# Layer norms of the graph front and behind the experts: the normalizing pass moved from VectorE to ScalarE

## What is computed

```python
def _layernorm(x, axis=-1, eps=1e-05):
    m = jnp.mean(x, axis=axis, keepdims=True)
    v = jnp.var(x, axis=axis, keepdims=True)
    return (x - m) / jnp.sqrt(v + eps)
...
x = x + _L0_gnn_ref(_layernorm(x), ...)   # three graph layers over 40000 edges
x = x + _L0_ffn_ref(_layernorm(x), ...)   # 16 experts, 3 chosen per token, and a shared one
x = x + _L1_gnn_ref(_layernorm(x), ...)   # graph convolution and kernelized attention
x = x + _L1_ffn_ref(_layernorm(x), ...)   # sparse choice of 128 of 1024
```

## Time and profile before

| | |
|---|---|
| median of three runs | 1318.26 us (1315.52 to 1320.05) |
| the profiled execution | 1312.12 us |
| its span, first to last instruction | 1310.4 us |
| TensorE busy (matmuls) | 1233.0 us, 94% |
| VectorE busy | 530.4 us, 40% |
| ScalarE busy | 442.3 us, 34% |
| GpSimd busy | 196.8 us, 15% |
| granted TensorE clock, mean | 0.984 of full |

### The profile page before, as it was taken

How to read it: one execution, slowest core, us unless ns; L and a number is a source line. 1 busy time by engine, 2 the same in 40 slices (tenths; PEclk the granted TensorE clock), 3 DMA queues, 4 the chain that set the end, 5 groups by cost and what they waited for, 6 DMA issues and landing times.

```text
span 1310.4 us, 19216 instructions
## 1 busy us (share of the span) xinstructions
PE 1233.0 (94%) x6568; PEld 820.9 (63%) x6569; DVE 530.4 (40%) x1399; ACT 442.3 (34%) x933; POOL 196.8 (15%) x209
## 2 busy tenths in 40 slices
PE   4999899999999899989999999999989999989797
PEld 3555485566456555468877887786565586564465
DVE  8999532111134335100000000001395355667894
ACT  7878532121212110011111111111122442338893
POOL 1000000000000007411111111111363000104480
PEclk9999999999999999999999999999999999989899
DMA  9200000000020110572164312664462000200011
GB/s 226 80 1 1 1 2 1 1 1 1 1 100 30 63 66 1 177 260 72 44 234 160 131 48 63 221 232 165 152 183 88 17 17 2 73 1 1 1 31 50
DMA packets 42977, 98.25 MB, mean 75 GB/s; under 512 B 4142, under 2 KB 6632, under 8 KB 41874
## 3 DMA queue, kind: packets, MB, share of 16 engines
q1 hardware_dynamic: 28642, 68.70, 15.7%
q0 software_dynamic: 6144, 16.45, 4.5%
q10 hardware_dynamic: 8112, 12.08, 2.5%
HBM read 81.02 MB, written 16.17 MB: 74 GB/s over the span
## 4 chain that ended last, share of the span: by engine, by line
PE 72%; DVE 12%; issue 4%; POOL 3%; ACT 3%; DMA 3%; ACTq 1%; DVEq 1%; POOLq 0%; SPq 0%
PE psum L481 36%; PE psum L1944 14%; PE psum L2034 7%; PE psum L1917 3%; POOL slot_tokens L760 3%; PE psum L2196 2%; PE psum L509 2%; PE psum L2062 1%; PE psum L2013 1%; DMA sb_blk<-slot_outs,sb_slot_i 1%; ACT sb_htok L883 1%; DVE sb_x_res L1322 1%; PE psum L2107 1%; DVE sb_stats L489 1%; PE psum L2135 1%
## 5 line engine op out<-in xcount | busy, mean ns | idle before, releaser
L481 PEld LDWEIGHTS psum<-sb_blk,sb_w_reg 128*128 128x128 f32 x1792 | 204.0, 192 | 12.7 <-issue 12.7
L481 PE MATMUL psum<-sb_blk,sb_w_reg 128*128 128x128 f32 x1792 | 205.2, 275 | 1.6 <-issue 1.6
L481 PE MATMUL psum<-sb_w_reg,sb_hT_conv 128*125 128x512 f32 (+1 forms) x376 | 167.2, 594 | 0.0
L1944 PE MATMUL psum<-sb_z_reg_r,sb_hT_conv_r 125*125 125x512 f32 x385 | 163.0, 423 | 0.4 <-DVE sb_z_last L1162 0.4
L1292 DVE TENSOR_TENSOR sb_blk<-sb_blk,psum 128x256 f32<-128x256 f32 x56 | 23.6, 421 | 277.0 <-ACT sb_blk L854 277.0
L481 PEld LDWEIGHTS psum<-sb_w_reg,sb_hT_conv 128*125 128x125 f32 (+1 forms) x376 | 68.4, 188 | 76.4 <-issue 75.8
L1944 PE MATMUL psum<-sb_htok_r,sb_hT_conv_r 125*125 125x512 f32 x285 | 112.9, 396 | 0.0
L481 PE MATMUL psum<-sb_hT_conv,sb_w_reg 128*128 128x416 f32 (+3 forms) x336 | 103.9, 467 | 0.8 <-ACT sb_hT_conv L515 0.8
L2034 PE MATMUL psum<-sb_w_reg,sb_blk 128*128 128x512 f32 x224 | 100.8, 592 | 0.0
L833 ACT CAST sb_hT_conv_r<-sb_a_reg 125x625 fp32r<-125x625 f32 x80 | 56.0, 715 | 116.0 <-PE psum L1944 111.9
L481 PEld LDWEIGHTS psum<-sb_hT_conv,sb_w_reg 128*128 128x128 f32 x336 | 64.8, 197 | 35.0 <-issue 31.2
(11 more groups left out here) (413 smaller groups left out, 1796.6 us busy)
## 6 DMA issues: line engine op xcount, KB each, us to landing
sb_hT_conv<-w_expert SPq DMA_DIRECT2D x7, 2048.0 KB, 9.8
sb_w_reg<-w_expert SPq DMA_DIRECT2D x6, 2048.0 KB, 18.7
sb_hT_conv<-w_expert SPq DMA_DIRECT2D x7, 1024.0 KB, 12.4
slot_outs<-sb_blk ACTq DMA_DIRECT2D x28, 256.0 KB
sb_w_reg<-w_expert SPq DMA_DIRECT2D x6, 1024.0 KB, 20.7
sb_w_reg<-w_gnn SPq DMA_DIRECT2D x1, 4096.0 KB
sb_w_reg<-w_qkv SPq DMA_DIRECT2D x1, 3072.0 KB, 21.6
slot_outs<-sb_blk ACTq DMA_DIRECT2D x1, 2560.0 KB, 10.5
```

Of the source, the lines that this page charges most:

```text
L481: ins = e.matmul(out, l, r, start=(n == 0), stop=(n == len(pairs) - 1))
L1944: ins = e.matmul(psum[0:TP, b, :], counts_at(l, 2 * i + n // NT)[:, s % HALF_T, :], z[s], start=(n == 0), stop=(n == len(pairs) - 1))
```

## The change

`vec_normed` is no longer called for the first and the third norm. In its place VectorE does `vec_shift`: it writes -mean * rstd over the variance of tile i, one number per token. ScalarE does `act_normed`: one activation Identity with scale `rstd` and bias -mean * rstd, 125 by 512 from `x_res` to `htok`, which raises `ln_out`.

```diff
+        def vec_shift(e, i):
+            e.wait_ge(v_own, rstd_step[i])
+            e.scalar_tensor_tensor(mv[:, i, 1:2], mv[:, i, 0:1], -1.0, rstd[:, i:i + 1], ALU.mult,
+                                   ALU.mult).then_inc(v_own, v.up())
+            shift_step[i] = v.n
+
+        def act_normed(e, n, i, out):
+            e.wait_ge(v_own, norm_steps[n][i])
+            e.activation(out, x_res[:, i, :], ACT.Identity, bias=mv[:, i, 1:2],
+                         scale=rstd[:, i:i + 1]).then_inc(ln_out, 1)
...
@@ ScalarE, the front, step t
                 for i in every(t, FIRST_LN + 1, 2):
                     act_std(e, 0, i)
+                for i in every(t, FIRST_LN + 3, 2):
+                    if i >= 3:
+                        e.wait_ge(turned, i - 2)
+                    act_normed(e, 0, i, htok[:, 7 + i % 3, :])
...
@@ ScalarE, behind the experts
                 for i in of_tiles(t, 0):
                     act_std(e, 2, i)
+                    act_normed(e, 2, i, htok[:, i, :])
...
@@ VectorE, vec_taken
                 if k == 1 and i >= 1:
                     vec_rstd(e, 2, i - 1)
-                    vec_normed(e, 2, i - 1, htok[:, i - 1, :])
+                    vec_shift(e, i - 1)
...
@@ VectorE, the front, step t
                 for i in every(t, FIRST_LN + 2, 2):
                     vec_rstd(e, 0, i)
-                for i in every(t, FIRST_LN + 3, 2):
-                    if i >= 3:
-                        e.wait_ge(turned, i - 2)
-                    vec_normed(e, 0, i, htok[:, 7 + i % 3, :])
+                    vec_shift(e, i)
...
@@ VectorE, behind the takes
             vec_rstd(e, 2, NT - 1)
-            vec_normed(e, 2, NT - 1, htok[:, NT - 1, :])
+            vec_shift(e, NT - 1)
```

More of the change, by code:

```diff
@@ L556, in build @@
         v, g_ = Count(), Count()
-        rstd_step = {}
+        rstd_step, shift_step = {}, {}
+        norm_steps = {}
         AFTER = (3, 2, 4)
@@ L1548, in vector @@
                     vec_rstd(e, 0, i)
-                for i in every(t, FIRST_LN + 3, 2):
-                    if i >= 3:
-                        e.wait_ge(turned, i - 2)
-                    vec_normed(e, 0, i, htok[:, 7 + i % 3, :])
+                    vec_shift(e, i)
                 for i in every(t, FIRST_Z + 6, Z_GAP):
                     vec_z(e, 0, i, z_bank(0, i), z_lo_rows)
+            norm_steps[0] = dict(shift_step)
             turns = e.value_load(more_i[0:1, 0:1], min_val=1, max_val=PASSES)
@@ L1763, in vector @@
             vec_rstd(e, 2, NT - 1)
-            vec_normed(e, 2, NT - 1, htok[:, NT - 1, :])
+            vec_shift(e, NT - 1)
+            norm_steps[2] = dict(shift_step)
             e.wait_ge(qkv_mm, 6)
@@ L2477, in build @@
         block.gpsimd(gpsimd)
+        block.vector(vector)
         block.scalar(scalar)
-        block.vector(vector)
         block.tensor(tensor)
```

## The result

| | kernel before | changed |
|---|---|---|
| median of 12 runs each | 1316.05 us (1313.54 to 1320.05) | 1321.84 us (1319.13 to 1323.75) |
| profiled execution (span) | 1312.12 us (1310.4) | 1322.41 us (1320.7) |
| mean granted clock in it | 0.984 | 0.977 |

The ratio is 1.0036, 95% interval 1.0025 to 1.0047: 3.3 to 6.2 us slower. I had forecast 3.1 us, 1321.4 on the median. The two medians lie 5.8 us apart, the ratio of the runs stands for 4.7. Timed again on another chip (the last experiment) the ratio was 1.0045, 1.0028 to 1.0062. One run of the experiment on the order of the programs took 4466 us and is left out of its ratio.

The account below looks back on a forecast made before the run. TensorE is 72% of the chain; VectorE is full in the front, where ScalarE would become the bound. Front +2.4 and behind the experts +0.7 give +3.1 us on 1318.26, so 1321.4, range 1314.5 to 1326.

Parts of the forecast that it names:

- Price of the norm on ScalarE: Each normed tile: 807 ns for 512 columns, from the 1250-column row; occupies ScalarE for 0.71 us (bounds 0.53 and 0.81).
- 0.61 us: Skill page's estimate per norm, 224 cycles plus one per column at 1.2 GHz; the front would lose 0.4 us.
- The shift: Front, VectorE: reciprocal and shift take 0.27 us instead of 0.51 per tile, a relief of 2.4 us for ten.
- ScalarE becomes the bound, its idle time is absorbed: Front: 7.1 us of norms against 4.4 us of idle time; ScalarE leaves 2.7 us later, replacing VectorE as bound.
- The rival in which the idle time stays: Front: square root waits persist, each norm delays the Relu by 0.71 us; +7.8 us in all, 1326.1; chance 0.17.
- Front: +2.4 us: Stretch from 19.85 to 51.07 us: ScalarE's 2.7 us delay, some 0.3 taken off; bounds -2.4 and +7.1.
- VectorE waits for TensorE up to 5 us: Expected profile sign in the front: VectorE's waits for TensorE rise from zero to some 5 us.
- Behind the experts: +0.7 us: 957 to 990 us: tile 7 turns 0.94 us later, 0.24 of idle time absorbs some; bounds -2.3 and +1.0.
- From the profiled execution to the median: Whole kernel: median of the runs shown taken as 6.1 us above the profiled execution, so 1315.2 becomes 1321.4.
- the start of my sum, 1318.26: Median of the kernel before, to which the forecast added 3.1 us for 1321.4.

Follow-up runs that it names:

- the last experiment: The changed kernel once more, unchanged, timed beside the kernel before on one chip: 1317.40 us, ratio 1.0045.
- the order of the programs: The kernel before with VectorE's program written ahead of ScalarE's, no engine's instructions changed: 1316.76 us, ratio 1.0002.
- half norms: Against the changed kernel: change in the front only, each of ScalarE's ten norms made in two halves of 256 columns: one run, 1315.28 us.
- five and eight tiles: Against the changed kernel: change in the front only, ScalarE norming just tiles 0 to 4 (1317.06 us, ratio 0.9997) or 0 to 7 (1314.96 us, ratio 1.0021).
- twelve Squares moved: Change in the front only, with one Square less on ScalarE and one comparison more on VectorE in twelve loop runs: 1314.44 us, ratio 1.0024.
- the change behind the experts alone: Against the changed kernel: front as before, only the norms behind the experts go to ScalarE: 1316.81 us, ratio 1.0015.
- the copy first: The change behind the experts only, with ScalarE's copy of tile i-2's turn ahead of the norm of tile i: 1319.17 us, ratio 1.0016.
- the padding: The changed kernel with 24 already met waits on ScalarE ahead of its norms behind the experts: 1321.68 us, ratio 1.0043.
- front alone: Against the changed kernel: ten norms in the front go to ScalarE, those behind the experts stay on VectorE: 1319.38 us, ratio 1.0026.

## Why the prediction was right, and where not

- **Price of the norm on ScalarE.** 807 ns forecast, 814 measured (802 to 832 for all twenty). Extrapolating the row with both pointer operands was right. The errata section of the Trainium skill's page "VectorE: DVE Perf Modes" would have given 0.61 us, as quoted ahead; the trace decides against it.
- **The shift.** 0.27 us with its reciprocal forecast, 0.24 measured.
- **ScalarE becomes the bound, its idle time is absorbed.** Right in the main. Busy 98% of the 31.2 us, waits for moments from 4.0 to 0.6 us. The rival in which the idle time stays would have been 7 us late; of the half norms' further work a fifth is absorbed. My sum took the idle time as one stock. The runs with five and eight tiles show it spent tile by tile, 0.4 us on average, which for all ten gives the same sum. And load is not the whole cause: with twelve Squares moved ScalarE had time left, and 1.05 of 1.9 us stayed.
- **Front: +2.4 us.** 2.5 to 2.7: 1.9 between the 11th and the 31st add, 0.6 to 0.8 in the nine steps up to the 10th. The loop ended 2.8 us later in the two profiles; the scatter of such a difference lies in the one step between, where the 11th add of five traces with the old front came between 32.01 and 33.33 us.
- **VectorE waits for TensorE up to 5 us.** Too much: 1.3 us by the releasers up to 51 us in the group that waits most, and 31.22 - 27.92 = 3.3 us of idle time in all.
- **Behind the experts: +0.7 us.** This step failed. The series of norm and copy is there, TensorE waits for `hT_in` ahead of tile 7 as described (0.83 and 1.77 us; forecast 2.7), and from the last gather to the squares the path is 0.52 us longer. What I had wrong is the start of that path. I held the last gather fixed at 979.45, and said that nothing moves up to tile 8's first take, although the gather's own row says that it waits 1.71 us for VectorE. VectorE's relief shortens that wait to 0.86, so the gather comes earlier, and from tile 4's first take to the squares nothing is lost (29.35 and 29.33 us, against 29.25 to 29.71). This rests on two traces of the change.
- **What I had not seen.** The 2.3 us in the end stage, which four of the five traces with the norms behind the experts on ScalarE have and none of the nine others. Without them the total would have been about 2.6 us. The 3.1 us forecast for the change hold 0.7 that isn't there and lack 2.3 that is.
- **From the profiled execution to the median.** I set the sum on an execution that lay 6.1 us under the median of three runs and took the difference as an offset. Over twelve runs before's median is 1316.05, only 3.9 above that execution. So the start of my sum, 1318.26, was 2.2 us too high, and this made up for most of what the change cost beyond the forecast: that 1321.4 lies 0.4 us from the measured 1321.84 is luck. The medians differ by 5.8 us where I said 3.1. Besides, I read the stretch from 957 to 990 us from an execution without the gap, and most executions of that time had one.

## What to carry to other kernels

Two engines that share a loop are one budget: an operation that takes 0.7 us of one, handed over to relieve the other by 0.24, cost 0.15 to 0.45 us each time here, although the taker had 4.4 us of idle time in the stretch. Idle time is spread over the steps; count it per step and not as one stock. Look for a stretch of the trace that reproduces to 0.01 us in kernels that shouldn't differ there, and read the edit's price in it. Count first which of the moved operations lie inside. Whole times that scatter by 8 us can't give it with a dozen runs. Profile the kernel before twice before reading a difference of 5 us as the change's doing.

## What the runs showed of the hardware

- **Gaps without a cause in the profile.** In six of the fourteen traces ScalarE stands idle for 5 to 9 us between 950 and 965 us, 4.4 to 7.5 of them with its input ready, while GpSimd's gathers run. In three others (the change behind the experts alone, the order of the programs, the copy first) TensorE halts instead, in the middle of a group of matmuls or transposes, two to five times for 0.4 to 1.6 us. In the four of the last chip and in before's first there is nothing of the kind, and before's medians go with it: 1311.73 us on that chip, 1316.33 and 1316.87 on the two others of the experiments. So a gap may come with the chip as well as by chance. ScalarE's copy of tile 1 waited 9.14 to 9.30 us in four different programs. That an engine's next instructions come late, behind the gathers' transfers, would look like this. It is a guess: the padding, meant to test it, moved the gap and settled nothing.
- **VectorE and GpSimd side by side.** The same 2.3 us in four executions: an operation on one column of VectorE at 1.98 instead of 0.16 us and GpSimd's long one at 2.84, or, in the ten others, VectorE undisturbed and GpSimd's at 3.92 to 3.93. The two started 22 to 34 ns apart in the first case, 4 to 18 in the second.
- **The clock.** Over the 83 runs of before on three chips the time falls as the mean granted clock of the run rises, by 9 us for each 0.01 (correlation -0.84 within a chip). Taking this line out leaves front alone at +3.6 us, behind the experts alone at +0.5 and the whole change at +3.9. That puts less on the change behind the experts alone than the 2.3 us that its trace loses in the end stage, and this disagreement stays open.
